# Encoder units: the first dense layer's biases move into ScalarE's relu, and the low parts of its values to GpSimd

## The reference

```
x = layernorm(x + o, n1w, n1b)                        # x1, after this unit's attention
ff = relu(x @ l1w.T + l1b) @ l2w.T + l2b              # 256 -> 1024 -> 256
return layernorm(x + ff, n2w, n2b)                    # y2, added to x with the gate's weight
```

## Time and profile before

| | |
|---|---|
| median of 3 runs | 774.62 us (772.61 to 774.81) |
| profiled execution, its own time | 775.13 us |
| its span (first to last instruction) | 773.3 us |
| busy in the span: PE, DVE | 711.8 us (92%), 623.7 us (81%) |
| busy in the span: ACT, POOL | 336.5 us (44%), 372.1 us (48%) |
| mean granted clock of PE | 0.969 |

### The profile page before, as it was taken

One profiled execution on the slowest core, in us unless ns is written; L12 is line 12 of the kernel. 1 busy time (PEld: TensorE's weight loads), 2 busy tenths in 40 slices (PEclk: granted clock), 3 DMA queues, 4 the chain that ended last, 5 costly groups with the idle time before them and its releaser, 6 DMA issues.

```text
span 773.3 us, 29161 instructions
## 1 busy us (share of the span) xinstructions
PE 711.8 (92%) x11020; PEld 565.4 (73%) x11020; DVE 623.7 (81%) x1803; ACT 336.5 (44%) x711; POOL 372.1 (48%) x637
## 2 busy tenths in 40 slices
PE   5788779999999999999999999999989999997897
PEld 4566457888888888888888888878766666665585
DVE  4798556778788878888797878788889889988885
ACT  5665224343434344343434343444445555553220
POOL 3778523354535354544545353544435544547344
PEclk9789689999999999999999999999999999999899
DMA  8974200000000000000000000000022221422111
GB/s 312 374 254 172 95 2 3 3 3 3 3 3 4 3 3 3 3 3 3 3 3 3 3 4 3 3 10 17 27 74 64 94 87 63 136 80 76 36 56 35
DMA packets 24800, 41.00 MB, mean 53 GB/s; under 512 B 3871, under 2 KB 16809, under 8 KB 24411
## 3 DMA queue, kind: packets, MB, share of 16 engines
q1 hardware_dynamic: 23240, 37.13, 14.1%
q0 software_dynamic: 704, 1.71, 0.8%
q10 hardware_dynamic: 726, 0.30, 0.2%
HBM read 30.60 MB, written 8.91 MB: 51 GB/s over the span
## 4 chain that ended last, share of the span: by engine, by line
PE 69%; DVE 16%; issue 6%; POOL 4%; ACT 3%; DMA 1%; POOLq 0%; DVEq 0%; ACTq 0%
PE ps L519 7%; PE ps L513 6%; PE ps L521 6%; PE ps L520 6%; PE ps L719 6%; PE ps L661 4%; DVE mx L1551 4%; PE ps L737 4%; PE ps L775 4%; PE ps L776 4%; PE ps L777 4%; PE ps L663 3%; PE ps L662 3%; PE ps L773 2%; PE ps L653 2%
## 5 line engine op out<-in xcount | busy, mean ns | idle before, releaser
L1160 ACT ACTIVATE pT<-ps 128x1024 f32<-128x1024 f32 x96 | 93.0, 1021 | 122.4 <-PE ps L719 122.4
L1551 DVE TENSOR_REDUCE mx<-ps 128x16 f32<-128x2048 f32 x48 | 109.5, 2281 | 1.0 <-PE ps L680 1.0
L2108 POOL TENSOR_TENSOR y<-y,vec 128x256 f32<-128x256 f32 x32 | 23.2, 725 | 171.5 <-DVE y L1317 171.5
L775 PE MATMUL ps<-xh,w_hi 128*128 128x128 bf16 x512 | 99.5, 220 | 0.0
L776 PE MATMUL ps<-xl,w_hi 128*128 128x128 bf16 x512 | 99.4, 220 | 0.0
L777 PE MATMUL ps<-xh,w_lo 128*128 128x128 bf16 x512 | 99.4, 219 | 0.0
L2013 POOL TENSOR_TENSOR rs<-rs,cst 128x1 f32<-128x1 f32 x132 | 73.3, 555 | 10.3
L2011 POOL TENSOR_TENSOR rs<-mv,cst 128x1 f32<-128x1 f32 x132 | 27.8, 210 | 100.6 <-DVE mv L1314 93.5
L519 PE MATMUL ps<-w_hi,hh 128*128 x256 | 69.9, 273 | 0.0
L520 PE MATMUL ps<-w_hi,hl 128*128 x256 | 69.8, 273 | 0.0
L521 PE MATMUL ps<-w_lo,hh 128*128 x256 | 69.8, 273 | 0.0
(11 more groups left out here) (365 smaller groups left out, 2432.3 us busy)
## 6 DMA issues: line engine op xcount, KB each, us to landing
vec<-in_w SPq DMA_DIRECT2D x16, 384.0 KB, 5.7
stage<-in_w SPq DMA_DIRECT2D x16, 384.0 KB, 4.9
vec<-in_vec SPq DMA_DIRECT2D x4, 896.0 KB, 6.7
vec<-in_tw SPq DMA_DIRECT2D x12, 256.0 KB, 2.9
ctxc<-in_ctx SPq DMA_DIRECT2D x19, 128.0 KB, 2.4
comb<-x SPq DMA_DIRECT2D x16, 128.0 KB, 1.7
comb<-x1b SPq DMA_DIRECT2D x16, 128.0 KB, 2.1
out<-x SPq DMA_DIRECT2D x16, 128.0 KB, 2.3
```

Of the source, the lines that this page charges most:

```text
L775: mm(dst, w(w_hi, c, j), xh[:, c, :], start=False, stop=False)
L1160: A(pT[:, 8 * a:8 * a + 8, :].rearrange("p h q -> p (h q)"), ps[:, 2 * a:2 * a + 2, :].rearrange("p g k -> p (g k)"), ACT.Exp, scale=SCALE ...
L1551: nc.vector.tensor_reduce(mx[:, :], att.rearrange("p g s k -> p (g s) k"), AX.X, ALU.max, negate=True).then_inc(m_max, 1)
```

## The change

- The bias products of hidden (line 773) are gone. The biases come as columns in a new tile bcols (16 KB, one DMA); POOL copies the 8 columns of a unit's expert into bunit, a ring of four, once per block (unit_bias).
- relu becomes five ACT instructions: four of 128 x 128 with a bias column each, into a float32 buffer hf, and then, after a wait for the fourth, a copy of hf into the bf16 hh. There is one hf for each half; the one of half 1 lies in the upper half of h.
- h_low moves from DVE to POOL, which can't read PSUM and reads hf. For half 1 it stands behind the root for norm2 and ahead of affine2 in the block of its unit; for half 0 it stands in the next block, behind the roots and ahead of affine1.
- On POOL, y_bias moves from ahead of affine1 to behind x1_bias. On ACT, oo(n) (the high part of o) moves ahead of relu(f, 1).
- PE waits for the low part of half 0 only ahead of second(g, 0), and second(g, 1) waits for relu's half 0 in its stead.
- At the start two of the four DMAs of bias rows are gone, with their two splits on ACT and DVE. DVE also waits for bcols ahead of the statistics of the fourth pair.

```diff
@@ -78,8 +78,10 @@
-B_QK = DFF
-B_ALL = DFF + 2 * D
+B_QK = 0
+B_ALL = 2 * D
+B_COLS = FC
+RING = 4
...
@@ -144,6 +146,9 @@
+        bcols = sb("bcols", [128, E * B_COLS])
+        bunit = sb("bunit", [128, RING, B_COLS])
+        hf_a = sb("hf_a", [128, 512])
...
@@ -208,6 +213,7 @@
+        hf = (hf_a, h[:, 512:1024])
...
@@ -259,6 +265,7 @@
+        bcols_in, hf_ready, bunit_ready = x_in2, x_in1, b1_zero
...
@@ -338,8 +345,7 @@
-        b1f = [(0, 512, v[0:NROW, :, :].rearrange("p h k -> p (h k)")), (512, 512, qk[0:NROW, :]),
-               (B_QK, D, khm[0:NROW, :, :, :].rearrange("p c s k -> p (c s k)").bitcast(f32)),
+        b1f = [(B_QK, D, khm[0:NROW, :, :, :].rearrange("p c s k -> p (c s k)").bitcast(f32)),
...
@@ -388,6 +394,7 @@
+            sp.dma_start(bcols[:, :], bc_d).then_inc(bcols_in, 16)
...
@@ -768,11 +775,9 @@
                 def w(t, c, j):
                     return t[:, ds(base + (W_L1 + 512 * half + 128 * j + c * DFF), 128)]
                 for j in range(4):
-                    b0 = 512 * half + 128 * j
                     dst = ps[:, 7 - half, 128 * j:128 * j + 128]
-                    mm(dst, b1hl[:, b0:b0 + 128], row_of(e), start=True, stop=False)
                     for c in range(KC):
-                        mm(dst, w(w_hi, c, j), xh[:, c, :], start=False, stop=False)
+                        mm(dst, w(w_hi, c, j), xh[:, c, :], start=(c == 0), stop=False)
                         mm(dst, w(w_hi, c, j), xl[:, c, :], start=False, stop=False)
                         last = mm(dst, w(w_lo, c, j), xh[:, c, :], start=False, stop=(c == KC - 1))
                 last.then_inc(h_b if half else h_a, 1)
...
@@ -781,6 +786,8 @@
                 if half == 1:
                     pe.wait_ge(hl_b, u + 1)
+                    pe.wait_ge(hh_a, u + 1)
+                else:
                     pe.wait_ge(hl_a, u + 1)
                 j0 = 4 * half
                 last = split_products(ps[:, 7, 0:D], lambda j: hh[:, j0 + j, :], lambda j: hl[:, j0 + j, :],
...
@@ -943,7 +950,7 @@
-            pe.wait_ge(b1_ready, 4)
+            pe.wait_ge(b1_ready, 2)
...
@@ -1119,7 +1126,7 @@
-                    act.wait_ge(b1_in, 16 * 4)
+                    act.wait_ge(b1_in, 16 * 2)
...
@@ -1175,8 +1182,16 @@
             def relu(u, half):
                 act.wait_ge(h_b if half else h_a, u + 1)
-                A(hh[:, 4 * half:4 * half + 4, :], ps[:, 7 - half, :].rearrange("p (c k) -> p c k", k=128),
-                  ACT.Relu).then_inc(hh_b if half else hh_a, 1)
+                act.wait_ge(bunit_ready, 1 + u + 1)
+                if u > 0:
+                    act.wait_ge(hl_b if half else hl_a, u)
+                for j in range(4):
+                    k = 4 * half + j
+                    last = A(hf[half][:, 128 * j:128 * j + 128], ps[:, 7 - half, 128 * j:128 * j + 128], ACT.Relu,
+                             bias=bunit[:, u % RING, k:k + 1])
+                last.then_inc(hf_ready, 1)
+                act.wait_ge(hf_ready, 16 + u * 2 + (1 if half else 2))
+                copy(hh[:, 4 * half:4 * half + 4, :], hf[half].rearrange("p (c k) -> p c k", k=128)).then_inc(hh_b if half else hh_a, 1)
             def block(n, kp):
...
@@ -1190,10 +1205,10 @@
                     x1_hi(f)
                 if kp is not None:
                     prep(kp, 2 * KC if isinstance(kp, int) and kp >= B else KC)
+                if attends(n):
+                    oo(n)
                 if encodes(f):
                     relu(f, 1)
-                if attends(n):
-                    oo(n)
                 shift(m)
                 if encodes(f):
                     relu(f, 0)
...
@@ -1425,7 +1440,7 @@
-                        dve.wait_ge(x_in2, 16)
+                        dve.wait_ge(x_in2, 32)
...
@@ -1592,11 +1607,6 @@
                    ALU.subtract).then_inc(x1T_split, 1)
-
-            def h_low(u, half):
-                dve.wait_ge(hh_b if half else hh_a, u + 1)
-                stt(hl[:, 4 * half:4 * half + 4, :], ps[:, 7 - half, :].rearrange("p (c k) -> p c k", k=128), 0.0,
-                    hh[:, 4 * half:4 * half + 4, :], ALU.max, ALU.subtract).then_inc(hl_b if half else hl_a, 1)
...
@@ -1715,16 +1725,12 @@
                     y_low(kp[0], 2 * KC if isinstance(kp[0], int) and kp[0] >= B else KC)
-                if encodes(f):
-                    h_low(f, 1)
                 if attends(n):
...
                         stats1(n)
-                if encodes(f):
-                    h_low(f, 0)
                 if encodes(g):
...
@@ -1854,6 +1860,7 @@
+            dve.wait_ge(hl_b, UNITS)
...
@@ -2096,6 +2103,16 @@
                 pool.wait_ge(l1_g, u + 1)
                 tt(x1[:, :], x1[:, :], vec[:, ds(base + V_B1, D)], ALU.add).then_inc(x1_ready, 1)
+            def h_low(u, half):
+                pool.wait_ge(hh_b if half else hh_a, u + 1)
+                tt(hl[:, 4 * half:4 * half + 4, :], hf[half].rearrange("p (c k) -> p c k", k=128),
+                   hh[:, 4 * half:4 * half + 4, :], ALU.subtract).then_inc(hl_b if half else hl_a, 1)
+
+            def unit_bias(u):
+
+                cols = bcols[:, ds(digit(words_pool[u // WORD], u % WORD) * B_COLS, B_COLS)]
+                nc.gpsimd.tensor_copy(bunit[:, u % RING, :], cols).then_inc(bunit_ready, 1)
+
             def x1_bias(u, slot, base):
                 pool.wait_ge(x1_ready, u + 1)
...
@@ -2116,16 +2133,23 @@
                     rstd(1, n, l1_var, l1_veps, l1_rstd)
                 if kp is not None:
                     y_root(kp)
+                if encodes(n - 2):
+                    h_low(n - 2, 0)
+                if encodes(f):
+                    affine1(f, ex(-1))
+                    x1_bias(f, 1 - slot, ex(-1))
                 if causal(m):
                     x_bias(m - UNITS, 1 - slot)
                 else:
                     y_bias(m, km, 1 - slot, ex(1))
-                if encodes(f):
-                    affine1(f, ex(-1))
-                    x1_bias(f, 1 - slot, ex(-1))
                 if encodes(n - 3):
                     rstd(2, n - 2, l2_var, l2_veps, l2_rstd)
+                if encodes(f):
+                    h_low(f, 1)
+                if encodes(n - 3):
                     affine2(n - 3, ex(-3))
+                if encodes(n + 2):
+                    unit_bias(n + 2)
             def tw(c, j):
                 pool.wait_ge(tw_hi, c + 1)
...
@@ -2149,6 +2173,8 @@
+                if b == 1:
+                    h_low(UNITS - 1, 0)
...
@@ -2180,6 +2206,8 @@
+            pool.wait_ge(bcols_in, 32)
+            unit_bias(0)
...
@@ -2282,8 +2310,8 @@
-    b1 = cat([cat([f0["lin1_b"], f0["in_proj_b"][:, :2 * D]], axis=1),
-              cat([np.zeros(DFF, np.float32), at["bq"], at["bk"]])[None, :]])
+    b1 = cat([f0["in_proj_b"][:, :2 * D], cat([at["bq"], at["bk"]])[None, :]])
+    bc = f0["lin1_b"].reshape(E * B_COLS, 128).T
...
```

More of the change, by code:

```diff
@@ L123, in served, with encoder_kernel @@
     return not isinstance(b, int) or 0 <= b < B
-def encoder_kernel(nc, x_d, ctx_d, mask_d, maskt_d, w_d, wc_d, vec_d, vc_d, b1_d, gw_d, gb_d, sw_d, sv_d, tw_d, tvec_d, tg_d, tb_d,
+def encoder_kernel(nc, x_d, ctx_d, mask_d, maskt_d, w_d, wc_d, vec_d, vc_d, b1_d, bc_d, gw_d, gb_d, sw_d, sv_d, tw_d, tvec_d, tg_d, tb_d,
                    ib_d, it_d, cst_d, kst_d, pos_d, out, comb_d, ytok_d, keys_d):
@@ L1436, in _ @@
                 if i == 4:
-                    dve.wait_ge(b1_ready, 4)
+                    dve.wait_ge(b1_ready, 2)
                     for slot in range(2):
@@ L2299 @@
         "maskt": a["mask_Bx1xS2_ik1"].reshape(B, S).T,
-        "w": w, "wc": wc, "vec": vec, "vc": vc, "b1": b1,
+        "w": w, "wc": wc, "vec": vec, "vc": vc, "b1": b1, "bc": bc,
         "gw": f0["gate_w"].T.reshape(KC, 128, E).transpose(1, 0, 2), "gb": f0["gate_b"][None, :],
```

## The result

| | before | changed |
|---|---|---|
| median of 4 runs each, us | 774.71 (772.61 to 775.07) | 809.86 (809.13 to 811.88) |
| profiled execution, its own time and span, us | 775.13 and 773.3 | 809.13 and 807.3 |
| mean granted clock of PE | 0.969 | 0.974 |

The ratio is 1.045, 95% interval 1.0431 to 1.0469. The forecast was 801 us with 786 to 815 around it: the direction held and so did the mechanism in the prep blocks; the cost came out 9 us too small.

What follows compares the result with a forecast made beforehand. The prediction took PE from out_proj to second(g, 0)'s end, then DVE from sum2 to ool, as the bound. It summed 775.1 + 29.2 - 1.0 - 0.9 - 0.9 = 801.5, hence 801 us, range 786 to 815.

Steps and rivals of the forecast that it cites:

- The bound: Block time: PE from out_proj to second(g, 0)'s end, then DVE from sum2 to ool, 4.17 us; removed products gain 0.
- The rival by which PE is the bound (760): All blocks: the 8 products drop out of each and y_of's wait is slack, 774.6 - 14.3 = 760; chance 7%.
- The term of 0.45 us a block for PE: PE in hidden: 8 bias products at 0.056 us, 0.45 us a unit, but hidden beside DVE's chain.
- y_of's wait: Prep blocks: DVE's y_of waits for POOL's late y_bias, starting 2.79 us later; 2.0 us a block, 29.2 us in all.
- order alone: POOL in prep blocks, without arrears: y_bias's late place costs 1.15 us each, 15 x 1.15 = 17 us.
- The blocks without prep: No y_of or root of y there; x1 ready about 2 us in, PE wants it at 3.1: no cost.
- the credit for time: POOL in blocks without prep: the longer prep block before gives it time, so x1 is ready at about 2 us.
- that price for y_of: DVE and POOL block each other: y_of takes 0.85 us, not 0.41, 6.6 us more in all, 808; chance 13%.
- The ends: Savings outside the steady blocks: 1.0 us at the start, 0.9 for affine1 in block 31, 0.9 in blocks 31 and 32.
- The 0.9 us that the missing products should have given in blocks 31 and 32: PE may be late there with mask products; removal gives up to 0.45 us each, 0.9 taken (0 to 0.9).
- hidden was to end before mtile in prep blocks: PE in prep blocks: hidden, though waiting for x1_low, was still to end before mtile.
- that rival: PE's clock falls as PE stands in prep blocks, stretching its part 0.5 to 1.7 us a block: 818; chance 7%.

Runs made afterwards that it cites:

- e1: Kernel before with hidden's bias products left out and nothing in their place: 775.28 us, ratio 0.9997.
- e2: Kernel before with only POOL's order changed, y_bias behind x1_bias: 788.14 us, ratio 1.0152.
- e5: Changed kernel with two buffers for y, DVE waiting for the shared expert's weights only at batch 1: 788.22 us, ratio 1.0167.
- e9: Changed kernel with h_low of half 0 alone back on DVE, behind the statistics of y: 792.50 us, ratio 1.0222.
- e10: Changed kernel with h_low of half 0 on POOL in two instructions of 128 x 256: 810.11 us, ratio 1.0447.
- e12: Kernel before with two y buffers, POOL's order root, root of y, affine1, y_bias, x1_bias, one projection_qk group early in blocks without prep: 773.02 us, ratio 0.997.
- e11: Changed kernel, h_low on DVE (half 0 behind y's statistics), two y buffers, y_bias between affine1 and x1_bias, one early projection_qk group without prep: 768.57 us, ratio 0.991.
- e4: Changed kernel with h_low back on DVE, half 0 ahead of y's statistics, and POOL's old order: 782.60 us, ratio 1.0082.
- e7: Changed kernel with h_low back on DVE, half 0 behind y's statistics, and POOL's old order: 772.56 us, ratio 0.9957.

## Why the prediction came out as it did

**The bound.** Right. Out_proj is released by DVE's ool, and DVE's chain starts with sum2; e1 shows the products' removal at 0 as forecast. The rival by which PE is the bound (760) is out. The term of 0.45 us a block for PE was mis-sized: e1 measured 0.19 to 0.21. It did no harm, since none of it counted in the blocks.

**y_of's wait.** Right in place and cause. y_bias was to end 5.12 us into the prep block and ends at 5.35 in block 22. The block was to grow by 2.0 and grew by 2.06, but that it is so near is in part luck. In the mean y_of starts 3.13 later (at 5.35 and not 2.22) where 2.79 were forecast, and sum2 2.23 later where 1.97 were; 0.14 of it came back between sum2 and ool's end. The two parts of the wait were shown apart: e2 is the order without any new work (0.92 a block), e5 the new work without the wait. The forecast's "order alone", 1.15 a block or 17 us, is another thing than e2: its sum has h_low(g, 0) with 1.11 us in it. In block 2, without affine2 in the queue, it was 0.87 and not 1.15.

**The blocks without prep.** This is the step that failed: "the longer prep block before gives it time, and x1 is ready about 2 us behind the block's start ... No cost there". x1 was ready at 3.15, and its transposes, which PE reaches at 3.10, started at 3.36; 0.21 a block, 3 us in all. e9 shows that it is x1: with it at 2.72 the others are back at 13.22. Without the credit for time my own durations give 2.74: h_low(f, 1) 3.65 us ahead of the block (390.69 against 394.34), then 1.11 + 1.59 + 0.15 + 0.79 + 1.11 + 0.91 + 0.73. The credit was wrong because the prep block's delay lies ahead of hidden: hh comes late by as much as the block's end does, and POOL gains no time on it. h_low(f, 1) starts at 428.29, 3.55 us ahead of the block from 431.84 us, where 3.69 lie between 412.63 and 416.32. That is 0.7 of the miss and 0.1 for the later start. The other 0.33 is the wait of affine1 for a norm of x1 that is held beside h_low(g, 0); 2.74 + 0.1 + 0.33 = 3.17. In e10, where the norm is held less, the others are at 13.25. I had taken that price for y_of, where it did not come (0.42 us), and not for the norm that lies beside the new instruction. The Trainium skill (SBUF — State Buffer, Who interferes with whom) says, of DVE's modes that use two ports, that whoever issues first has the shared pair of ports for its whole instruction and the other one blocks, and it says that a tensor_tensor of DVE's with both inputs in SBUF contends with GpSimd's reads. The changed kernel and e10 (DVE's norm held to the end of POOL's instruction) and e9 (POOL's root held to the end of DVE's tensor_tensor) agree.

**The ends.** Forecast 2.8 us saved, measured 0.1 lost. At the start 0.4 went and not 1.0, and even the 0.4 can't be told from none: block -1 starts at 93.0 to 94.5 us in the four profiles with the old start (before, e1, e2, e12) and at 92.4 to 94.7 in the ten with the new one. In block 31 I had let affine1's bias go from the queue and had not put h_low(g, 0) in its place, where it took 1.37 us beside y_of's 1.25. The wait of the earlier trace rows grew from 0.89 to 1.34:

```profile
551.60 0.41 PE L520 MATMUL ps<-cst,x 128*128 128x128 f32 x2 [1.34 <-POOL x L2104]
```

The 0.9 us that the missing products should have given in blocks 31 and 32 is not to be seen in their lengths (0.1 and 0.4 longer).

So of the span's 34.0 us against a forecast of 26.4, 3.0 are the other blocks, 2.9 the ends, and 1.6 the prep blocks (28.8 + 1.96 against 29.2). The remaining 1.3 of the 8.9 between 801 and 809.9 is how each profiled execution stands to its median.

**The rest.** hidden was to end before mtile in prep blocks. It ended after it: mtile was ready at 10.86, its transpose came at 11.32. It costs 0.03 us only, since ool comes at 11.19 (out_proj 0.20 behind ool, 0.17 before). ACT, the answer to the earlier trace rows:

```profile
410.48 0.37 ACT L1068 CAST ooh<-ps 128x256 bf16<-128x256 f32 x1 [3.34 <-PE ps L520]
410.75 1.15 ACT L1190 ACTIVATE h<-ps,bunit 128x128 f32<-128x128 f32 x4
411.93 0.62 ACT L1068 CAST hh<-h 128x512 bf16<-128x512 f32 x1
```

The four activations took 1.15 us against 1.11 forecast, the copy 0.62 as in the earlier trace rows, and between them there was 0.03 and not 0.1. By an estimate from the figures of the Trainium skill (ScalarE: Activation LUTs, What ACT_TABLE_LOAD costs) the four would have been 1.26; the measurement lies between, nearer to the row. The clock stayed at 1.00 in the prep block, although PE stands there, and in the whole stretch from 128 to 530 us, so that rival is out.

## What to carry to other kernels

Work taken off an engine pays only where that engine sets the end: find what releases the next stage, and if it is another engine, have something ready to put into the hole before the work is taken away (e1 0 us; 0.12 us a block without prep in e11 against e12). Work moved to an idle engine joins a queue: list what stands behind it there, down to the last small operation, and who waits for each; here two instructions of 1.16 us a block and a changed order cost 35 us. And an instruction that has come to wait longer for another engine should stand behind everything that others wait for (e4 to e7, 10 us for the place of one call).

## What the runs showed of the hardware that was not expected

**PE's pace.** Three products of hidden, whose weights lie at an address from a register, come every 0.17 us in the prep block of e5, and every 0.24 in that of the changed kernel, where PE had waited 0.68 us for DVE just ahead. Clock 1.00 in both. The changed kernel and then e5:

```profile
423.40 0.44 PE L520 MATMUL ps<-cst,y 128*128 128x128 f32 x2 [0.68 <-DVE klm L1561]
423.81 0.23 PE L780 MATMUL ps<-xh,w_hi 128*128 128x128 bf16 x1
...
424.05 0.23 PE L780 MATMUL ps<-xh,w_hi 128*128 128x128 bf16 x1
...
424.32 0.23 PE L780 MATMUL ps<-xh,w_hi 128*128 128x128 bf16 x1
```

```profile
409.57 0.22 PE L784 MATMUL ps<-xh,w_hi 128*128 128x128 bf16 x1
...
409.74 0.22 PE L784 MATMUL ps<-xh,w_hi 128*128 128x128 bf16 x1
...
409.91 0.22 PE L784 MATMUL ps<-xh,w_hi 128*128 128x128 bf16 x1
```

From hidden's first weight product to its last it is 3.90 us in the changed kernel's prep blocks, 3.86 in e9's and 3.89 in e2's (56 products there), all with y_of late; 3.07 in e5's and, with 56 products, 3.24 in those of the kernel before. The length of the wait just ahead doesn't set it: it is 0.2 to 0.7 us in the changed kernel and only 0 to 0.3 in e2. And e1 has groups at 0.24 with no wait at all ahead of hidden. The time of the whole hardly shows it: the four activations of half 1 start 5.43 us ahead of the prep block's end in the changed kernel and 5.48 in e5. What slows PE is open; no run takes it apart.

**Ports between DVE and POOL.** The hold goes in both directions, and even an operation on a single column is held: 0.19 us became 0.59 (e9). In the other direction 0.41 became 1.24.
